# Cross attention and its output projection as one stage: queries on partitions, block-diagonal keys, transposed probabilities

## What is computed

```
q = (xq @ wq.T + bq)   # heads of 32
k = (xkv @ wk.T + bk)
v = (xkv @ wv.T + bv)
scores = einsum('bhqd,bhkd->bhqk', q, k) / sqrt(hd)
scores = scores + bias[None]
attn = softmax(scores, axis=-1)
out = einsum('bhqk,bhkd->bhqd', attn, v)
y = y + out @ w_out.T + b_out
```

## Time and profile before

| | |
|---|---|
| median of three runs | 3227.7 us |
| the profiled execution, its own time | 3224.82 us |
| its span (first to last instruction) | 3222.8 us |
| mean granted TensorE clock | 0.905 of full |
| PE busy in the span | 2912.8 us (90%) |
| DVE, ACT, POOL busy | 1600.9, 1164.6, 292.4 us |
| cross attention, from its first DMA issue | at 1947.62 us |
| output projection, from its first DMA issue | at 2283.32 us |
| feed-forward, from its first DMA issue | at 2442.46 us |

### The profile page before, as it was taken

The page is one execution under the profiler, slowest core; times in us unless marked ns, Lnnn a source line. Parts: engine busy times, 40 slices in busy tenths (PEclk is TensorE's granted clock), DMA queues, the critical chain, the costliest instruction groups (busy, mean ns, idle before and its releaser), DMA issues. The chain is left out here.

```text
span 3222.8 us, 42342 instructions
## 1 busy us (share of the span) xinstructions
PE 2912.8 (90%) x12544; PEld 1873.8 (58%) x12544; DVE 1600.9 (50%) x3785; ACT 1164.6 (36%) x2119; POOL 292.4 (9%) x330
## 2 busy tenths in 40 slices
PE   5699979999999999999986986999576999999998
PEld 4588854444444444444434774555254777777777
DVE  4244457777777777778735652222353222222211
ACT  1033213555555555555552431333211222222222
POOL 1300010000000000000002113200135300000000
PEclk7899979999999999999998995555688999999999
DMA  9445452223332222222208847754683100000000
GB/s 289 92 153 188 170 153 63 60 60 78 76 81 67 61 61 61 61 62 60 60 24 211 236 148 180 168 129 103 166 238 106 41 1 27 27 26 26 27 13 14
DMA packets 148453, 311.51 MB, mean 97 GB/s; under 512 B 42797, under 2 KB 67997, under 8 KB 137610
## 3 DMA queue, kind: packets, MB, share of 16 engines
q1 hardware_dynamic: 143434, 294.15, 33.2%
q0 software_dynamic: 4800, 14.68, 1.6%
HBM read 205.18 MB, written 110.15 MB: 98 GB/s over the span
## 5 line engine op out<-in xcount | busy, mean ns | idle before, releaser
L972 ACT ACTIVATE sa_pr<-sa_st 128x512 f32<-128x512 f32 (+3 forms) x1280 | 612.1, 532 | 565.3 <-DVE sa_st L1035 324.9
L940 PE MATMUL sa_ov<-sa_pr,sa_v 128*33 128x512 f32 (+3 forms) x2560 | 537.4, 541 | 0.0
L1021 DVE TENSOR_REDUCE sa_part<-sa_mp 128x1 f32<-128x512 f32 (+3 forms) x768 | 411.4, 582 | 119.4 <-PE sa_mp L921 118.5
L931 PE MATMUL sa_st<-sa_q,sa_k 97*128 97x512 f32 (+3 forms) x1280 | 439.4, 413 | 23.5 <-ACT sa_pr L972 13.7
L931 PEld LDWEIGHTS sa_st<-sa_q,sa_k 97*128 97x128 f32 x1280 | 216.6, 189 | 322.4 <-ACT sa_pr L972 207.8
L921 PE MATMUL sa_mp<-sa_k,sa_q 96*128 96x512 f32 (+3 forms) x1280 | 373.6, 386 | 24.6 <-DVE sa_mp L999 19.1
L1018 DVE CUSTOM_DVE_ANT_0 sa_mp<-sa_mp,sa_ub 128x512 f32<-128x512 f32 (+3 forms) x512 | 317.9, 664 | 76.6 <-PE sa_mp L921 71.7
L105 PE MATMUL ff_f<-ff_ln_hi,ff_w 128*128 128x512 f32 x1024 | 343.5, 396 | 2.9 <-DVE ff_ln_lo L532 2.9
L1771 DVE TENSOR_TENSOR ff_hl<-ff_hf,ff_hh 128x512 fp32r<-128x512 f32 x128 | 92.2, 720 | 479.6 <-ACT ff_hh L1753 479.6
L1716 PE MATMUL ff_o<-ff_w,ff_hh 128*128 128x512 f32 x1024 | 323.9, 397 | 3.1 <-DVE ff_hl L1771 3.1
L921 PEld LDWEIGHTS sa_mp<-sa_k,sa_q 96*128 96x128 f32 x1280 | 232.5, 193 | 95.9 <-DVE sa_part L1021 24.9
(11 more groups left out here) (195 smaller groups left out, 3318.4 us busy)
## 6 DMA issues: line engine op xcount, KB each, us to landing
sa_q<-scratch_q SPq DMA_DIRECT2D x192, 128.0 KB, 4.5
sa_k<-scratch_k SPq DMA_DIRECT2D x192, 128.0 KB, 4.6
ca_q<-scratch_q SPq DMA_DIRECT2D x48, 512.0 KB
scratch_q<-qkv_qst SPq DMA_DIRECT2D x32, 512.0 KB, 2.8
scratch_k<-qkv_qst SPq DMA_DIRECT2D x32, 512.0 KB, 2.8
scratch_q<-sao_qst SPq DMA_DIRECT2D x32, 512.0 KB, 2.9
scratch_v<-qkv_vst SPq DMA_DIRECT2D x8, 1056.0 KB, 5.2
sa_v<-scratch_v SPq DMA_DIRECT2D x16, 528.0 KB, 6.6
```

What stands on the lines that cost most here:

```text
L931: pe.matmul(st[bank(u, h)][:, 0:w], ks[n.par][:, h, kb * P:(kb + 1) * P], qs[n.par][:, h, g * GW + c0:(g + 1) * GW], start=True, stop=True ...
L940: last = pe.matmul(ov[64 * h:64 * h + VW, c0:GW], vs[n.par][:, kb, h, :], pr[:, u % 4, h, 0:GW - c0], start=(u in opens), stop=(u in ends))
L972: act.activation(pr[:, u % 4, h, 0:w], st[bank(u, h)][:, 0:w], ACT.Exp, scale=SCALE).then_inc(s["exp"], 1)
L1021: dve.tensor_reduce(to, tile, AX_X, ALU.max).then_inc(s["red"], 1)
```

## The change

`attention(..., False)` and `attention_out("ca", ...)` are replaced by one stage, `cross_attention`. The layout of the work is new.

- A slot q (0 to 31) is one block of 512 tokens by one chunk of 128 query features, which is four heads. `score` multiplies 128 queries (stationary, all four heads' features on 128 partitions) by a block-diagonal key matrix `kd` of 128 by 4·77 = 308, so the scores of four heads come out side by side with queries on partitions, once, in three fp32r products.
- DVE adds the bias for near rows, takes the maxima over keys (128x4), scales and negates them (`shift`); ACT takes four exponentials of 128x77 with the negated maximum as a per-partition bias operand (`exponent`); DVE sums and inverts; POOL multiplies the probabilities by the reciprocals.
- PE transposes the probabilities (`turn`, 16 per slot, plain float32), ACT copies them out (`evacuate`), PE multiplies by the values, four heads at output partitions 0, 32, 64 and 96 (`values`); ACT and DVE split the result in hi and lo (`high`, `low`), and `project` and `residual` finish as before. Attention outputs, sums and reciprocals no longer go through DRAM.
- The stages of one slot are staggered: scores run LEAD = 2 slots ahead, the projection of token block e runs LAG = 5 slots behind. The loops are written out in Python, with no hardware loop.
- POOL's weight splits are interleaved, one job per slot. The DRAM table `ca_T`, its DMA in the encoder and the rounded identity are gone.

```diff
-                attention(k, "ca", dr, ident, identr, False, split)
-                attention_out(k, "ca", io, dr, ident, wo, y1.ap(), y2.ap(), None)
+                cross_attention(k, io, dr, ident, wo, split, y1.ap(), y2.ap())
...
-            sp.dma_start(dr["ca_T"].ap(), bass.AP(dr["rows"], 2 * GL + S - 1, [[W, H], [-1, S], [1, 2 * P]])).then_inc(s["gx"], 16)
...
-            act.activation(identr[:], ident[:], ACT.Copy).then_inc(s["idr"], 1)
```

The new PE program (`n` is `4 q + i`, a block of 128 queries, in `score`, and `4 q + j` in `turn`; `slots()` is `range(-2, 37)`):

```diff
+            def score(n):
...
+                waits(pe, s["exp"], n - 2)
+                t = slice(i * P, (i + 1) * P)
+                for x, (a, c) in enumerate(((0, 0), (0, 1), (1, 0))):
+                    last = pe.matmul(sps[n % 3][:, 0:W], qb[q % QB][:, a, t], kd[b][:, c, m, :],
+                                     start=(x == 0), stop=(x == 2))
+                last.then_inc(s["score"], 1)
+
+            def turn(q, j):
+                n = q * HC + j
+                waits(pe, s["copied"], n - 1)
+                for i in range(TT):
+                    if j == 0:
+                        pe.wait_ge(s["normal"], TT * q + i + 1)
+                    last = pe.transpose(tps[n % 2][0:S, i * P:(i + 1) * P], pq[:, (TT * q + i) % (PB * TT), j, :], ident[:])
+                last.then_inc(s["turned"], 1)
...
+                pe.wait_ge(s["copied"], HC * (q + 1))
+                waits(pe, s["low"], q)
+                for j in range(HC):
+                    last = pe.matmul(ov[j * HD:(j + 1) * HD, :], cv[:, b, m * HC + j, 0:HD], pt[:, q % 2, j, :],
+                                     start=True, stop=True)
+                last.then_inc(s["value"], 1)
...
+            for q in slots():
+                e = q - LAG
+                for half in range(2):
+                    if has(q):
+                        for j in (2 * half, 2 * half + 1):
+                            turn(q, j)
+                    if has(q + LEAD):
+                        for i in (2 * half, 2 * half + 1):
+                            score(TT * (q + LEAD) + i)
+                    if has(e, NE):
+                        project(e, (2 * half, 2 * half + 1))
+                if has(q - 1):
+                    values(q - 1)
```

ACT, DVE and POOL:

```diff
+            def exponent(n):
+                act.wait_ge(s["shift"], n + 1)
+                r, q = n % (PB * TT), n // TT
+                waits(act, s["turned"], HC * (q - PB + 1))
+                for j in range(HC):
+                    last = act.activation(pq[:, r, j, :], sps[n % 3][:, j * S:(j + 1) * S], ACT.Exp,
+                                          bias=ng[:, r, j:j + 1], scale=SCALE)
+                last.then_inc(s["exp"], 1)
...
+            for q in slots():
+                if has(q - 2):
+                    high(q - 2)
+                for half in range(2):
+                    if has(q):
+                        for j in (2 * half, 2 * half + 1):
+                            evacuate(q, j)
+                    if has(q + LEAD):
+                        for i in (2 * half, 2 * half + 1):
+                            exponent(TT * (q + LEAD) + i)
...
+            for q in slots():
+                if has(q - 2):
+                    low(q - 2)
+                for half in range(2):
+                    if has(q + LEAD):
+                        n = TT * (q + LEAD) + 2 * half
+                        shift(n)
+                        shift(n + 1)
+                        sums(n)
+                        sums(n + 1)
+                        inverse(n)
+                    if half == 0 and has(q - LAG - 1, NE):
+                        residual(q - LAG - 1)
...
+                if has(q + LEAD):
+                    for n in blocks(q + LEAD):
+                        pool.wait_ge(s["inverse"], n // 2 + 1)
+                        r = n % (PB * TT)
+                        pool.tensor_tensor(pq[:, r], pq[:, r], inv[:, r].unsqueeze(2).to_broadcast([P, HC, S]),
+                                           ALU.mult).then_inc(s["normal"], 1)
```

More of the change, by code:

```diff
@@ L1050, in _ @@
             run(dve, N, slot)
[L1054 to L1085, removed]
@@ L1088 @@
[L1088 to L1119, removed]
@@ L1122, in shares @@
[L1122 to L1133, removed]
-    nc = k.nc
[L1139 to L1164, removed]
-    with k:
[L1166 to L1175, removed]
-        st = [k.ps(f"{name}_st{i}", [P, 2, GW]) for i in range(2)]
-        mp = [k.ps(f"{name}_mp{i}", [P, 512]) for i in range(2)]
-        ov = [k.ps(f"{name}_ov{i}", [P, GW]) for i in range(2)]
-        s = k.sems(name, "init in0 in1 in2 in3 rest0 rest1 scores bias exp av out st0 st1 chunk red max row0 row1")
-        block = k.block()
-        def place(n):
-            return Step(n.t, n.i // B, n.unroll // B), n.i % B
@@ L1239, in _ @@
-            for n in range(ahead):
-                row(Step(0, n, unroll, nbuf), 0)
-                if n < ahead - 1:
-                    row(Step(0, n, unroll, nbuf), 1)
-            def slot(n, left):
-                if left >= nbuf - 1:
-                    load(n + (nbuf - 1))
-                if left >= ahead - 1:
-                    row(n + (ahead - 1), 1)
-                for g in range(GB):
-                    store(n, g)
-                    if g == row_after and left >= ahead:
-                        row(n + ahead, 0)
@@ L1253, in _, with load_q @@
[L1253 to L1260 removed]
+            def load_q(q):
+                g, m, _ = chunk(q)
+                waits(sp, s["score"], TT * (q - QB + 1))
+                sp.dma_start(raw(qb[q % QB][:]),
+                             dr["qk"][0][:, m * P:(m + 1) * P, g * GW:(g + 1) * GW].rearrange("l p t -> p l t"))\
+                  .then_inc(s[f"q{q % QB}"], 16)
@@ new lines, in project @@
+            def project(e, cs):
+                g, i = e // TT, e % TT
+                if cs[0] == 0:
+                    if e == 0:
+                        pe.wait_ge(split.s["lo"], KC)
+                    pe.wait_ge(s["low"], KC * (g + 1))
+                    waits(pe, s["done"], e - 1)
+                t = slice(i * P, (i + 1) * P)
+                for c in cs:
+                    for x, (a, ww) in enumerate(((oh, wo_h), (oh, wo_l), (ol, wo_h))):
+                        last = pe.matmul(ops[e % 2][:], a[:, g % 2, c, t], ww[:, c, :],
+                                         start=(c == 0 and x == 0), stop=(c == KC - 1 and x == 2))
+                if cs[-1] == KC - 1:
+                    last.then_inc(s["product"], 1)
@@ new lines, in high @@
+            def high(q):
+                g, m, _ = chunk(q)
+                act.wait_ge(s["value"], q + 1)
+                waits(act, s["product"], TT * (g - 1))
+                act.activation(oh[:, g % 2, m, :], ov[:], ACT.Copy).then_inc(s["high"], 1)
+            for q in slots():
+                if has(q - 2):
[7 more added lines that the diff above has]
+                            exponent(TT * (q + LEAD) + i)
@@ new lines, in residual @@
+            def residual(e):
+                dve.wait_ge(s["product"], e + 1)
+                dve.wait_ge(s["added"], e + 1)
+                dve.tensor_tensor(y[:, e % YB], ops[e % 2][:], y[:, e % YB], ALU.add).then_inc(s["done"], 1)
+            for q in slots():
+                if has(q - 2):
[10 more added lines that the diff above has]
+                        residual(q - LAG - 1)
```

334 lines of the change are left out of this document (137 added, 197 removed).

## The result

The changed kernel takes **3056.0 us** (median of 4 runs, 3053.0 to 3058.9) where the kernel before, on the same chip, takes 3227.5: a ratio of 0.9465, 95% interval 0.9453 to 0.9477. The forecast was 3043, its range 3005 to 3110. The direction holds, and so does the loop that was forecast, but for one link of it that another engine holds up; the stage is 13 us longer than forecast.

A forecast was written before the change was run, and what follows sets the result against it. PE, then DMA in the projection, bounded old cross attention; the DVE-ACT-DVE loop would set the new pace. Its steps summed to 310 us against 494.8, 185 us less: a median of 3043 us, range 3005 to 3110.

The forecast's parts named there:

- the loop that was forecast: New cross attention: the loop DVE-ACT-DVE, not any engine's busy time, sets the pace, 4.0 us a half, 8.0 a slot.
- slots 0 to 4: Cross-attention slots with no projection yet, PE still at the low clock: 8.2 us each, 41 us.
- slots 5 to 29: Cross-attention slots with projection, at 8.0 us and 1.0 more in the four computing near blocks: 205 us.
- signs of being wrong: PE without idle time in slots 5 to 29, clock row staying at 5, or `ca_t` waiting for POOL's multiplications.
- Small ones are 0.18: DVE's small instructions in the loop, the scaling to negated maxima among them, were priced at 0.18 us each.
- rival 3: POOL binds while it has weight jobs, multiplications at 1.4 us: 26 us more, 3070 us; 7%.
- PE's prices: PE at full clock: scores 0.142 us, transposes 0.109, projections 0.234, values 0.87 per slot; 7.1 us a slot.
- rival 1: The clock stays low in the new stage; PE bounds each slot with 13.3 us, whole about 3190 us; 10%.
- Rival 2: Value products at four column positions do not overlap, 3.4 us a slot: 47 us more, 3090 us; 6%.
- Rivals 3 and 4: Besides rival 3, the fourth: POOL's multiplications make it slower than before, at 3.5 us each 3283 us; 3%.
- ScalarE: ACT's exponentials start 0.217 us apart by the rows; by the skill's page 0.251, total 12 us higher.
- Outside the stage: Edits outside cross attention were costed at nothing; if the cover were not there, a gain of at most a few us.

The follow-up runs named there:

- e1: Changed kernel with the row maxima written to unused PSUM columns and the scaling reading them there: 3022.7 us, ratio 0.9366.
- e2: Changed kernel without POOL's 128 multiplications by the reciprocal sums, PE waiting for the reciprocals instead: 3039.5 us, ratio 0.9410.
- e3: Changed kernel with one of each score's three matmuls kept, the two with a low part left out: 3056.9 us, ratio 0.9466.
- e4: Changed kernel with DVE's row sums and reciprocals of a pair of tiles moved behind the next pair's maxima: 3017.5 us, ratio 0.9345.
- e5: Changed kernel with the edits of e1 and e4 together: 3014.0 us, ratio 0.9343.
- e6: Changed kernel with the edits of e1, e4 and e3 together: 2995.6 us, ratio 0.9285.
- e8: Changed kernel with the output projections of all 32 tiles moved behind the last attention slot: 3128.1 us, ratio 0.9692.
- e11: The changed kernel as it is, run once more as a yardstick: 3056.9 us, ratio 0.9468.

## Why the prediction was right, and where it was off

The stage runs from 1950.78 to 2274.30 us (the first issue of the feed-forward), 323.5 us against 494.8 before and 310 forecast. By the steps of the sum, with DVE's first row sum of a slot as its boundary (the first such comes 2.4 us behind the first shift, which the second row holds):

| step | forecast | measured |
|---|---|---|
| start, to the first shift | 17 | 18.0 |
| slots -2 and -1 | 15 | 17.8 |
| slots 0 to 4 | 41 | 38.1 |
| slots 5 to 29 | 205 | 218.9 |
| slots 30 to 36 and the exit | 32 | 30.7 |
| sum | 310 | 323.5 |

**The loop: right.** "This loop DVE-ACT-DVE, not any engine's busy time, sets the pace" is what e1 to e4 show from four sides. Of the signs of being wrong none is there: PE is idle for a tenth of the middle, the clock is up, and the transposes wait for ACT's copies (5.0 us in the stage) and never for POOL's multiplications. The loop's price without hold-ups, which e1 shows, is 3.76 us a half and not 4.0: exponentials start 0.208 us apart (0.217 forecast), and DVE's next instruction starts some 0.08 before the record of the last one ends.

**The term that was mis-sized: "Small ones are 0.18".** That holds for an instruction with POOL silent. In a steady slot the four take 0.47, 0.17, 0.49 and 0.81 us, 1.3 more than four short ones; 1.0 of that comes through to the slot of 7.52. So 8.0 became 8.5 by an overestimate of 0.5 and an omission of 1.0. This is most of the 13.9 us in slots 5 to 29; the four slots with near blocks (9.7 to 10.4 instead of 9.0) are the rest. That the two errors have opposite signs is luck, and part of why the total came so near. So is the row of slots 0 to 4: it was forecast as PE's work at the low clock, 8.2 us a slot, without the bias additions of two of them; the slots were 7.5 to 7.8 us long with the clock up.

The trace of before holds the warning. Its feed-forward has the same kind of instruction, a scaling of 128x4 from SBUF to SBUF, eight times: six take 0.17 us, and the two that run beside POOL's work take 0.33 and 0.65, ending 0.02 to 0.03 us behind a POOL instruction (here at 2497.04 and 2497.01):

```profile
2496.38 0.65 DVE L492 TENSOR_SCALAR ff_ln_std<-ff_ln_mv 128x4 f32<-128x4 f32 x1
2496.27 0.73 POOL L441 TENSOR_TENSOR ff_w<-ff_w_stage,ff_w 128x256 fp32r<-128x256 f32 x1
```

The 0.18 was taken from a reciprocal, and the step moved POOL's 128 multiplications into the middle of the loop. The prediction asked only whether POOL would be late (rival 3), not what POOL would hold.

The Trainium skill has the rule, on the page "SBUF — State Buffer", section "Who interferes with whom": VectorE and GpSimd share one pair of ports, and a VectorE instruction in a mode that uses both pairs contends for it with GpSimd; whoever issues first has it for the whole instruction. It names `tensor_scalar` among the operations that can do so, and says that `tensor_reduce` never contends on trn2. The traces agree: ends 0.02 us apart, 0.81 to 0.29 us with the instruction halved, 0.16 with the source in PSUM. Its page "VectorE: DVE Perf Modes", section "Mode 2×_2P — use both read ports for one tensor", says that both read ports then serve one tensor, for instructions with a single source, and that this needs SBUF and not PSUM. The scaling fits this, and in e1 it no longer does. The row sums (SBUF to SBUF, one source, a `tensor_reduce`) were not held up, as the first page says: the 43 beside POOL's work took 0.466 us on average, the others 0.474. That the mode is what takes the ports no trace shows by itself; the hold, its end and its two remedies are what the runs show.

**PE's prices: right.** Transposes start 0.109 us apart, scores 0.142, projections 0.232, against 0.109, 0.142 and 0.234. PE's slot is 7.37 by e5, 7.1 forecast; the four heads' values hold most of the difference, 1.1 us with what they wait for against 0.87.

**The clock, rival 1: false here.** Full clock came at 1983 us, 40 us ahead of the first projection (2022.86). Ahead of the rise PE had done scores and only eight transposes; behind it, up to the first projection, it did scores, transposes and value products, at a mean of 0.95. So the projections, to which the prediction tied the full clock, were not needed for it: its reason was wrong where its answer was right. The stretch from 1983 to 2020 had 0.81 to 1.00 in the profiles with all of PE's products; where two of three score products are left out it had 0.59 in e3 and 0.88 in e6. With the projections taken out of the slots (e8) the middle ran at a mean of 0.89. What in PE's work decides stays open, and of the rule that the prediction cited from the Trainium skill ("TensorE: Matmul & The Clock Gate", Part 4), that transposes don't count, no run here is a test: none has transposes alone. In e8 the lower clock cost nothing, since its steady slots stayed at 7.50 us whatever the clock was.

**Rival 2: false.** The four heads' value matmuls lie on each other; the eight records of a slot span 1.07 us:

```profile
2185.91 1.07 PE L1208 MATMUL ca_o<-ca_pt,ca_v 77*32 77x512 f32 x8
```

**Rivals 3 and 4: false in their price.** A multiplication with a broadcast operand takes 701 ns, less than the 0.91 taken and far from the 3.1 from which it would have turned the sign. What POOL did cost came by another way.

**ScalarE.** The Trainium skill's page "ScalarE: Activation LUTs", section "What ACT_TABLE_LOAD costs", by the prediction's reading would have put exponentials 0.251 us apart; the trace has 0.208 (the median between 2130 and 2200 us). Its total, 12 us more, came close to the measured one for a reason that is not its own.

**Outside the stage: no gain seen, as forecast.** The stage begins 3.2 us later than before. The eleven profiles of the experiments, which share the code ahead of the stage, have its first issue anywhere from 1947.9 to 1955.1 us, so 3.2 us can be spread between executions. But none of them is ahead of the one profile of before (1947.62), so that a cost of a few us there is not ruled out.

## What to carry to other kernels

When no engine is full, write down the loop that passes through all of them and price its smallest instruction beside what the other engines do at that moment, not by its size. A tiny VectorE instruction from SBUF to SBUF in such a loop can be held until GpSimd's running instruction ends, as this scaling was (the row sums and the reciprocals were not): put its source in PSUM, or cut the neighbour into shorter pieces. And test an edit's worth again once the bound has moved: the same eight matmuls a slot were worth nothing and then 18 us.

## What the runs showed that I had not expected

- A VectorE scaling of 128x4 takes 0.16 us from PSUM beside any work of GpSimd, and 0.17 to 1.2 us from SBUF; where it is long, it ends (but for 3 of 107) at most 0.04 us behind GpSimd's running instruction.
- Writing the maxima to PSUM instead of SBUF costs the reduction 10 ns (466 to 476).
- A GpSimd multiplication of 128x308 with a broadcast second operand takes 701 ns; its addition of 128x512 takes 1277. Per element that is 2.28 and 2.49 ns: nothing is seen of a cost of the broadcast.
- The kernel before had such holds too, where both sources of a VectorE instruction are in SBUF: of the 32 multiplications of 128x512 by the reciprocals in its output projection, the 12 beside GpSimd's work took 1.49 us on average, the other 20 0.68.
- Two GpSimd additions of 128x256 take 1.42 us against 1.27 for one of 128x512, yet made the kernel 14 us faster (3043.0 against 3056.9 of e11).
